# Copies of queries and keys allowed three list units earlier past a held output, projections three units behind the copies

## What is computed

```
mod = (silu(c) @ wmod) -> sa, ca, ga, sb, cb, gb     # ga, gb kept at least 0.25 in size
h   = layernorm(x) * (1 + ca) + sa
q, k, v = split(h @ qkv_w.T)                         # 16 heads of 16
out = softmax(q k^T / 4) v ; out = out @ proj_w.T + proj_b
x   = x + ga * out
h   = layernorm(x) * (1 + cb) + sb
per batch: recon_n = relu(h W_enc[n] + b_enc[n]) W_dec[n] + b_dec[n]  (n = 0..7)
           top = argmin_n mean((recon_n - h)^2)
x   = x + gb * (h W_base + b_base + relu(h W_down[top] + b_down[top]) W_up[top] + b_up[top])
```

## The kernel before

| group | its two qk steps | its 12 copies | threshold while held | held turns in between |
|---|---|---|---|---|
| 4 | 33.75, 42.75 | 43.5 to 45.75 | 46 | none |
| 5 | 51.75, 57.75 | 3 at 58.5, 9 from 62.25 to 63.75 | 62 | 59.25 to 64.5 |
| 6 | 66.0, 67.5 | 71.25 to 73.5 | 78 | 68.25 to 70.5 |
| 8 | 93.75, 97.5 | 6 at 98.25 and 99.0, 6 from 103.5 | 110 | 99.75 to 102.75 |
| 10 | 126, 128.25 | 3 at 129.0, 9 from 135.75 | 142 | 129.75 to 135.0 |
| 12 | 159, 161.25 | 3 at 162.0, 9 from 166.5 | 174 | 162.75 to 165.75 |
| 14 | 190.5, 191.25 | 3 at 192.0, 9 from 198.75 to 200.25 | 198 | 192.75 to 198.0 |
| 15 | 202.5, 204.0 | 207.75, 208.5 | 206 | none |

## Time and profile before

### The profile page before, as it was taken

How to read it: one execution, slowest core, us unless ns; L and a number is a source line. 1 busy time by engine, 2 the same in 40 slices (tenths; PEclk the granted TensorE clock), 3 DMA queues, 4 the chain that set the end, 5 groups by cost and what they waited for, 6 DMA issues and landing times.

```text
span 1004.2 us, 16485 instructions
## 1 busy us (share of the span) xinstructions
PE 962.7 (96%) x5794; PEld 480.8 (48%) x5794; DVE 813.2 (81%) x1657; ACT 661.7 (66%) x1295; POOL 284.4 (28%) x391
## 2 busy tenths in 40 slices
PE   6989999999899999999999999999999999999998
PEld 5444344343344445554454454545454455644476
DVE  4789989899688887788888888788778788889455
ACT  2148787887577777667668786766657767666831
POOL 4210133022155241200336431300237413116320
PEclk9879999999899999999999999999999999999999
DMA  6850051242550513242223511404424311132001
GB/s 180 141 92 23 12 107 45 56 95 71 80 96 12 96 34 66 44 85 81 70 87 60 85 44 45 75 13 78 130 70 80 58 29 35 38 96 77 29 6 48
DMA packets 47890, 66.93 MB, mean 67 GB/s; under 512 B 12139, under 2 KB 32112, under 8 KB 47796
## 3 DMA queue, kind: packets, MB, share of 16 engines
q1 hardware_dynamic: 46572, 65.00, 29.9%
q0 software_dynamic: 384, 0.79, 0.5%
q10 hardware_dynamic: 852, 0.09, 0.1%
HBM read 27.48 MB, written 12.59 MB: 40 GB/s over the span
## 4 chain that ended last, share of the span: by engine, by line
PE 77%; DVE 9%; ACT 5%; issue 2%; POOL 2%; DMA 2%; SPq 1%; ACTq 0%; DVEq 0%; POOLq 0%
PE pE L811 25%; PE pO L811 22%; PE pX L811 18%; PE pM L811 11%; DVE mx L1293 4%; ACT P L1118 2%; DMA QO<-lo 1%; ACT h1T L1159 1%; DVE h2f L1454 1%; ACT h2f L1205 1%; ACT hi L1175 1%; DVE lo L1374 1%; SPq L1867 0%; DVE junk L1430 0%; DMA P<-in_wmod 0%
## 5 line engine op out<-in xcount | busy, mean ns | idle before, releaser
L1293 DVE TENSOR_REDUCE mx<-pM 128x1 f32<-128x512 f32 x1006 | 629.7, 682 | 76.7 <-PE pM L811 71.4
L1118 ACT ACTIVATE P<-pE 128x512 f32<-128x512 f32 x996 | 526.7, 601 | 181.1 <-PE pE L811 177.8
L811 PE MATMUL pM<-KO,QO 48*128 48x512 f32 x1006 | 370.7, 455 | 6.8 <-DMA QO<-lo 3.3
L811 PE MATMUL pE<-QO,KO 50*128 50x512 f32 x996 | 349.2, 438 | 11.9 <-ACT h1T L1159 5.1
L811 PEld LDWEIGHTS pE<-QO,KO 50*128 50x128 f32 x996 | 164.9, 187 | 234.1 <-issue 125.1
L811 PE MATMUL pO<-P,V 128*17 128x512 f32 x2048 | 257.9, 598 | 5.1 <-ACT P L1118 5.1
L811 PEld LDWEIGHTS pM<-KO,QO 48*128 48x128 f32 x1006 | 164.3, 187 | 41.3 <-DVE mx L1293 28.8
L811 PEld LDWEIGHTS pO<-P,V 128*17 128x17 f32 x2048 | 40.5, 96 | 103.2 <-issue 88.1
L1695 POOL CAST mh<-mxc 128x16 fp32r<-128x16 f32 x32 | 6.5, 203 | 285.7 <-DVE mxc L1302 285.5
L811 PE MATMUL pX<-h1T,wqkv_s 128*128 128x512 f32 x112 | 59.2, 642 | 1.9 <-DVE lo L1374 1.5
L1754 POOL TENSOR_TENSOR Hs<-h2f,Hs 128x512 fp32r<-128x512 f32 x28 | 35.7, 1284 | 83.6 <-ACT Hs L1235 68.3
(11 more groups left out here) (301 smaller groups left out, 1023.4 us busy)
## 6 DMA issues: line engine op xcount, KB each, us to landing
outs<-osb SPq DMA_DIRECT2D x31, 256.0 KB, 2.9
KO<-hi SPq DMA_DIRECT2D x56, 128.0 KB, 4.0
QO<-hi SPq DMA_DIRECT2D x56, 128.0 KB, 5.1
x<-in_x SPq DMA_DIRECT2D x20, 256.0 KB, 3.6
out<-x SPq DMA_DIRECT2D x16, 256.0 KB, 2.1
AT<-outs SPq DMA_DIRECT2D x15, 256.0 KB
asum<-wsum SPq DMA_DIRECT2D x15, 256.0 KB
KO<-lo SPq DMA_DIRECT2D x28, 128.0 KB, 3.6
```

The source lines that it names most:

```text
L811: return e.matmul(o, lhsT, rhs, start=start, stop=stop)
L1118: e.activation(P[:, u % 3, j, :], bank(s), ACT.Exp).then_inc(*empties(s))
L1293: e.tensor_reduce(mx[:, hq % 2, k:k + 1, kh], bank(s), AX.X, ALU.max, negate=True).then_inc(*empties(s))
```

## The change

Two numbers of the planner. In `before()` a qk step of group gi now asks that the last copy of group gi-1 lies three units back in the list and not two. In the main loop the threshold from which copies go although an output's steps are waiting is three units lower: nine units, not six, before the group's maxima start.

```diff
     if kind == "qk":
 
-        return [(("ln1turn", b, 2 * a[1] + i), 1) for i in range(2)] + [(("moved", 4 * b + a[0] - 1), 2)]
+        return [(("ln1turn", b, 2 * a[1] + i), 1) for i in range(2)] + [(("moved", 4 * b + a[0] - 1), 3)]
...
-            if moving and (not held or u > 8 * SEQ.index((moving[0][1], 0)) - LEAD // 4 - 6) and (moving[0][1] < 3 or at >= 32 * (SEQ.index((moving[0][1] - 3, 1)) + 1)):
+            if moving and (not held or u > 8 * SEQ.index((moving[0][1], 0)) - LEAD // 4 - 9) and (moving[0][1] < 3 or at >= 32 * (SEQ.index((moving[0][1] - 3, 1)) + 1)):
                 out.append(moving.popleft())
```

## The result

| | before | after |
|---|---|---|
| median (13 runs each, beside each other) | 1007.31 us (1004.9 to 1011.82) | 1014.51 us (1012.15 to 1018.13) |
| profiled execution, span | 1006.01, 1004.2 us | 1013.36, 1011.6 us |
| mean granted clock | 0.988 | 0.985 |

The ratio is 1.0066, with a 95% interval from 1.0052 to 1.0079: slower by 6.6 us (5.2 to 7.9), where I had forecast 4.2 us less. The page of the kernel after answers to the earlier trace rows: busy times, then the chain by engine.

A forecast was written before the change was run, and what follows sets the result against it. PE was taken to bound the kernel, with time to gain only where it stalls or runs slowly. The terms -6.6 + 0.4 + 2.0 + 0 = -4.2 us took 1007.9 to 1003.7 us, range 1000.4 to 1008.6.

The forecast's parts named there:

- What bounds the kernel: PE, busy 962.7 of 1004.2 us; time is to be had only where it stands still or runs slowly.
- the stall of 6.6 us: Group 5's late last copy costs PE 3.17 us idle plus 3.42 of slow clock; issuing it earlier gives -6.6.
- hidden work: Rival, chance 0.20: another engine sets the pace in group 5's slow stretch, only 3.17 us comes back; 1007.1 us.
- The rows of maxima in place one: At unit 64, behind nine fresh copies: 0 by group 4's 4.6 us, 2.3 with the slowest copy; taken at 0.4.
- place one: Group 5: its nine copies follow `AT` directly, the last issued near 245.6 and not 255.67.
- `asum` in place one: Group 5: issued right behind the rows of maxima at 249.9, where before it was 251.81; not on the path.
- Place two: Group 14's nine copies, not late before, delay rows of maxima at unit 200: wait 0 to 5.4, taken at 2.0.
- the slower rival: Chance 0.07: rows come with the slowest copy at groups 5 and 14, clock falls: 2.3, 5.4, 3.4; +4.5, 1012.4 us.
- The reshuffle: Reordered steps after unit 201 add and remove no work: taken at 0, with -2 and +2 as ends.
- The second edit by itself is worth nothing.: The lag of three moves only group 15's projection, every other qk step being clear; it costs no wait either.
- The rule that I took from the Trainium skill: Small DMAs behind copies on a ring always pay the copies' landing: group 14's wait 1.7 or more, never 0.

The follow-up runs named there:

- b4_group14_split: Kernel before with only group 14's copies early, six of nine ahead of the rows of maxima and three behind: ratio 0.9998.
- a6_copies14: Kernel before with only group 14's nine copies moved early, order of all other steps unchanged: ratio 1.0052, +5.3 us.
- a5_turns: Kernel before with copies where they were; only the last projection and the steps after it ordered as in the kernel after: ratio 1.0027, +2.7 us.
- b2_group5_split: Kernel before with only group 5's copies early, six of nine ahead of the rows of maxima and three behind: ratio 0.9962.
- b1_rows_on_act: Kernel after with the rows of maxima of half groups 8 and 25 issued from ACT's queue, not SP's: 1.009 against the kernel before, +9.1 us.
- a4_thr: Kernel before with the first edit alone, thresholds three units lower and lag still two: ratio 1.0049, +4.9 us.
- a1_group5: Kernel before with only group 5's nine copies moved early, lag two: ratio 0.996, -4.0 us.
- a3_lag: Kernel before with the second edit alone, lag three and threshold as before: ratio 0.9963, -3.7 us.
- c1_split_again: Same list as b2_group5_split, timed again in more rounds against the kernel before: ratio 0.9938, 1001.72 us against 1006.89.
- a2_group14: Kernel before with group 14's nine copies early and the steps behind ordered as in the kernel after, group 5 unchanged: ratio 1.0073, +7.4 us.
- c3_lag_group6: Kernel before with the lag of three for group 6 alone, all other turns by the old rules: ratio 0.9984, -1.6 us.
- c2_both_parts: Kernel before with lag three everywhere and group 5's copies early, six ahead of the rows of maxima and three behind: ratio 0.9954, -4.6 us.

## Why the prediction was wrong, step by step

- **What bounds the kernel, and the stall of 6.6 us.** Right in mechanism: the copies follow `AT`, the stall goes, and the clock is whole in the 20 us behind. The slow clock wasn't hidden work: it came back. But 6.6 us is the stall's price in executions like the profiled one; where the clock had been low just ahead, the stall was 1.0 us and the cure gave 1.5 (last section).
- **The rows of maxima in place one, taken at 0.4.** Mis-sized. They took 7.2 us and PE waited 1.78. I leaned on group 4's 4.6 us as "just this way". It wasn't: what counts is when the last copy ahead lands. In group 4 it landed after 4.8 us (200.48 to 205.3), in `b4_group14_split` after 3.9, and 4.6 us was enough for the rows; here it took 8.3, and the rows 7.2. The sum -6.6 + 1.8 = -4.8 would have been near the -4.0 and -4.3 measured.
- **`asum` in place one.** The step "issued right behind the rows of maxima at 249.9" failed: I left out that it waits for `wsum` to land, which is a small DMA behind the same copies (247.56 to 254.87, 7.3 us). It cost nothing on PE, as I said of `asum` in general.
- **Place two, taken at 2.0 of 0 to 5.4.** The term that decided. PE's wait was 4.16, inside the bounds, and the working was right up to one number: the last copy ahead issued at 755.5, the rows there when it lands. I took a landing of 5.5 us from the earlier trace rows, where SP issues nothing but group 14's copies. Here the last copy took 8.0, and 755.5 + 8.0 - 759.3 = 4.2. `asum` and the load of `x`, 256 KB each, stand among the copies now; whether they make the difference no run tried. And the bounds for the place left out its second half: I gave the fall of the clock behind a wait of over 3 us (3.4) to the slower rival alone, though the earlier trace rows had shown it behind 3.17. 4.16 + 3.1 = 7.3 for 2.0; `a6_copies14` measured 5.3 by ratio and 6.5 by marks. The slower rival had this mechanism right in both places (1.8 for its 2.3, 4.2 for its 5.4, 3.1 for its 3.4), and its chance of 0.07 was far too low: I held against it that it needs the longest landing of all (9.2) twice, but 8.3 and 8.0 came near that in both places.
- **The reshuffle, taken at 0 with ends of 2.** The turns were right, the price wasn't: +2.7 (0.9 to 4.5) by `a5_turns`. I priced a moved step by its own duration. What counts is which bank and which DVE work stand ahead of it, far down the list, some 140 us behind unit 201.
- **"The second edit by itself is worth nothing."** Wrong in both ways. I asked if the lag binds in the changed list, not what it does alone: alone it is a cure of the same stall (-3.7), and with the threshold it decides between 199.5 and 201 for group 15.
- **The rule that I took from the Trainium skill** (DMA: Bandwidth & Descriptors, section Queues, rings and completion order). By it, I said, the wait would be 1.7 or more and never 0. 4.16 agrees, and so do the other places: each time the rows were there 0.1 to 0.9 us after the last copy ahead had landed (254.7 and 255.17 in place one, 760.4 and 760.55 in place two, 762.9 and 763.12 in `a6_copies14`, 252.3 and 253.21 in `b2_group5_split`). `b1_rows_on_act`, whose small DMAs weren't in the copies' ring, waited as long, so ring order is not needed for it. The rule's other half, an increment that lands only behind every earlier write of its DMA engine, fits that run too; no run separates it from plain sharing of the engines.

In sum: -6.6 + 0.4 + 2.0 + 0 = -4.2 became, by the traces, -4.0 (stall and rows together) + 6.5 + 4.3 = +6.8, with +6.6 timed.

## What to carry to other kernels

When copies are moved ahead of a small DMA, expect it when the last of them lands, and take that landing from a row with as many copies in flight, not from a median: 8.0 us here against 5.5. Another issuing engine didn't evade it. Price a PE wait together with the slow clock behind it whenever the profile of before shows that pair once, and put both into the forecast, not only into a rival. A late transfer can be cured by issuing it earlier or by asking for it later; in a list walked in order, either one moves steps far behind, and that is worth a price of its own.

## What the runs showed of the hardware

A DMA of 4 KB from SBUF to SBUF took 7.5, 7.6 and, from ACT's queue, 7.3 us from issue to use in place two, behind six `QO` copies of 128 KB, and 7.2 behind place one's nine copies. It took 5.9 behind six copies of which three were of `QO` (`b2_group5_split`), and no more than 4.6 behind three `QO` copies in `b4_group14_split`. From SP's queue it was there, wherever PE waited for it, 0.1 to 0.9 us after the last copy ahead had landed.

The clock fell to its lower level behind PE waits of 4.2, 3.2 and 1.7 us, for about 6.8 (10.2 in `a4_thr`), 6.8 and 3.4 us, but not behind the 1.78 and 1.35 us at unit 64 (kernel after and `a1_group5`). And it also fell without such a wait. In the profile of `a6_copies14`, whose list is that of the kernel before up to unit 195, the stretches ahead of the old stall and around it are these, then the PV that waits in the stall:

```profile
245.00:250.00 5.00, 5.00 (x16) 2.63 (x14) 3.44 (x9) 2.06 (x5) 4.01 (x4) 0.60 0.02 3
265.00:270.00 5.00, 4.03 (x28) 1.34 (x28) 2.67 (x5) 2.79 (x6) 0.00 (x0) 1.00 0.21 46
```
```profile
267.84 1.05 PE L811 MATMUL pO<-P,V 128*17 128x512 f32 x8 [0.97 <-ACT P L1118]
```

The clock was low from 246.0 to 252.8, before the stall. PE and ACT came to that place later, ACT waited 2.4 us for the copies and not 4.6, PE stood 0.97 us and not 3.17, and the clock stayed whole behind it. From half group 8's mark to 9's this execution takes 29.8 us, where the kernel before took 32.2 with the same list. Four more profiles have the fall near 245: `b1_rows_on_act`, `a3_lag`, `a4_thr` and `c1_split_again`. So place one's cure is worth one of two amounts. Without that fall the stretch goes from 32.2 us to 28.3 (after), 27.9 (`a1_group5`) and 27.2 (`b2_group5_split`); with it, from 29.8 to 28.3 (`a4_thr`, `c1_split_again`), which is 1.5. The timed medians mix the two kinds in shares that nobody counted.

Other falls behind no wait that the other executions don't have too are near 365 (`a2_group14`), 486 (`b2_group5_split`), 700 (`a1_group5`, `c3_lag_group6`), 897 (`a1_group5`) and 908 us (`a3_lag`, `c1_split_again`, `c2_both_parts`, `c3_lag_group6`). One list can so differ by 3 us from itself: the profiled spans of `c1_split_again` and `b2_group5_split`, one and the same list, are 1004.2 and 1001.2. That is why marks on both sides of a place were compared here, and not the ends of spans, and why even a pair of marks is one execution's account.
